# Cross-attention and soft mixture of experts: slot embeddings in the first steps, row scores between projections, key and query tiles in 104 rows, experts' weights behind the moves

## The chip, the cores and the metric

The kernel runs on one core of a Trainium2 chip. The metric is the device time of one execution in microseconds (us). TensorE (PE in the profile) multiplies, VectorE (DVE), ScalarE (ACT) and GpSimd (POOL) work on tiles, and SP only issues transfers. ACT and POOL issue transfers as well. The profile calls the loading of a stationary operand PEld.

## The reference

There are 16 batches of 100 query rows and 361 context rows of width 256. First `x = x + attention(layernorm(x), ctx, ctx)` with 16 heads of 16, then `x = x + ffn(layernorm(x))`, where the second part is a soft mixture of 16 experts with 64 slots each:

```python
q = query @ wq + bq;  k = key @ wk + bk;  v = value @ wv + bv
score = einsum('bhqd,bhkd->bhqk', q, k) / sqrt(HD) + (1.0 - mask) * -1e9
context = einsum('bhqk,bhkd->bhqd', softmax(score, -1), v)
x = x + context @ wo + bo
# ffn
x = _layernorm(x, norm_g, norm_b)
se = _layernorm(slot_embeds, slot_g, slot_b) * scale
logits = einsum('bnd,esd->bnes', x, se)
dispatch = softmax(logits, axis=1)
combine = softmax(logits over all e, s)
slots = einsum('bnd,bnes->besd', x, dispatch)
gate = gelu(slots @ Wg + bg);  up = slots @ Wu + bu
eout = (gate * up) @ Wd + bd
out = einsum('bns,bso->bno', combine, eout)
```

## The kernel before, in words

The program has three phases.

**Attention.** It is a pipeline over batches. Step t (from -3 to 17) works on several batches at once: keys and queries of batch t+3, values of t+2, row scores of t+1, probabilities of t, output of t-1. Each step has 24 slots, and a table gives the slot of every piece: `AT` for t from 0 on, `AT_FILL` for the three fill steps -3, -2 and -1. Every engine runs its own list in this order and waits on semaphores. Precision is kept by splitting values in a high and a low part, so keys and queries go out to DRAM (`k_parts`, `q_parts`) and come back as tiles `kt` and `qt`, in which one head of each half takes 48 rows of parts, 2 of mask and 2 of the maximum. The two halves (c = 0, 1) lie at rows 0 and 64.

Row scores (`scores(r)`, L697, tile `at_rows`) multiply one pair of heads, one matmul for each half in its own 50 rows; DVE takes the maximum (`head_max`, L485); after eight pairs the maxima are transposed, split and moved into rows of `qt` (`max_rows`, L257). Column scores (`scores_t`, L709, tile `at_cols`) then use all 116 rows at once, and ACT takes the exponential (`p_f`, L626), splits it (`p_h`, L631, and POOL `p_l`, L391), and PE multiplies by the values (L729).

Slot embeddings: their inputs are issued on SP in step -2 (`later_inputs`, L312 to L315); DVE takes the statistics in step 12 (L460 to L466) and normalises in step 13 (L473); POOL multiplies and adds the gains in steps 13 and 14 (L415, L418); PE transposes them in step 15 (L835) and ACT copies them (`seT`, L671).

**Routing** computes the logits and both softmaxes for each batch and is not touched but for `norm_g` and `norm_b`, which it reads.

**Experts.** Eight pairs of experts, each in two halves of the batch (h) and two experts (e): 32 units. A unit is gate and up (L1454), down (L1493), and between them slots of the next half (L1421) and combines of the previous half (L1428). DVE adds the bias into `eo` in two parts (g = 0, 1; L1359), SP moves `eo` to `eo_pair` (L1258), and the combine of the next half reads `eo_pair` after its first two gate-and-up blocks. POOL issues the weights of the next pair: `wd` and `bd` (L1164, L1165) when the last eo part is there, `wgu` (L1159) when the low parts of the former ones are made.

## Time and profile before

| | us |
|---|---|
| median of 3 runs | 1232.62 |
| lowest, highest | 1227.69, 1235.58 |
| the profiled execution, its own time | 1230.74 |
| its span | 1229.0 |
| mean granted TensorE clock | 0.934 |

The span is cut in three phases by lines: attention from 0 to 381 us, routing to about 528 us, experts to the end. The page shows busy time of each engine, and the same in 40 slices of 30.7 us, with the granted clock in tenths of 2.4 GHz. PE is busy for 89% of the span. "Idle before" in brackets is the time the engine stood still before a row and who released it.

### The profile page before, as it was taken

The page shows a single profiled execution, that of the slowest core. Times are in us where ns is not written, and L with a number is a line of the kernel's source. Part 1 is how long each engine was busy: PE and PEld are TensorE (multiplying, and loading weights), DVE is VectorE, ACT ScalarE, POOL GpSimd, SP SyncE. Part 2 cuts the span into 40 slices and gives each one's busy share as a digit, 9 for nine tenths or more (in the row PEclk, how much of TensorE's full clock was granted, in tenths as well). Part 3 has the DMA queues.
Part 4 walks back from the last instruction along what each step waited for, and adds up shares of the span by engine and source line. Part 5 has one row for each costly group of instructions (what it writes and reads, how often), then busy time and mean ns, then how long its engine had stood idle before and what let it go on. Part 6 is the DMA issues. An engine that isn't in the chain of part 4 may idle for free.

```text
span 1229.0 us, 22101 instructions
## 1 busy us (share of the span) xinstructions
PE 1094.6 (89%) x7172; PEld 865.6 (70%) x7172; DVE 701.0 (57%) x1250; ACT 576.1 (47%) x1079; POOL 344.7 (28%) x351
## 2 busy tenths in 40 slices
PE   5389899999785888789989989899899899999996
PEld 3256666666562544478878878788788788888885
DVE  5246677777734888644545645555555545555443
ACT  2147678778553888733323333333324334343321
POOL 5137777668772533210010100100100100100000
PEclk8659999999857999889999989999999999999998
DMA  7836576667301634432142232422422331423022
GB/s 176 193 73 167 134 158 164 150 147 165 81 1 35 172 101 107 124 126 62 39 124 72 60 103 70 100 82 63 133 70 55 107 87 38 124 70 75 20 62 71
DMA packets 114565, 121.74 MB, mean 99 GB/s; under 512 B 45096, under 2 KB 105188, under 8 KB 114516
## 3 DMA queue, kind: packets, MB, share of 16 engines
q1 hardware_dynamic: 102188, 80.69, 27.7%
q0 software_dynamic: 10688, 39.62, 10.7%
q10 hardware_dynamic: 1640, 0.80, 0.3%
q8 instruction: 28, 0.46, 0.2%
q14 instruction: 21, 0.17, 0.1%
HBM read 74.13 MB, written 29.93 MB: 85 GB/s over the span
## 4 chain that ended last, share of the span: by engine, by line
PE 53%; issue 3%; DVE 1%; ACT 1%; DVEq 0%; ACTq 0%
PE down L1493 15%; PE gate L1454 14%; PE up L1454 14%; PE mix L1428 5%; PE mix L1421 5%; DVE gate_sb L1336 0%; ACT hid_h L1399 0%; DVE hid_l L1341 0%; DVE slot_l L1309 0%; DVE wd_l L1347 0%; ACT gate_sb L1395 0%; ACT slot_h L1379 0%; DVE x L1318 0%; DVEq L1545 0%; DVEq L1335 0%
## 5 line engine op out<-in xcount | busy, mean ns | idle before, releaser
L1395 ACT ACTIVATE gate_sb<-gate,bgu 128x512 f32<-128x512 f32 x128 | 88.1, 688 | 249.8 <-PE gate L1454 236.3
L391 POOL TENSOR_TENSOR p_l<-p_f,p_h 121x800 f16<-121x800 f32 (+1 forms) x96 | 163.3, 1719 | 89.8 <-ACT p_h L631 89.8
L1399 ACT ACTIVATE hid_h<-gate_sb 128x512 fp32r<-128x512 f32 x128 | 80.9, 632 | 183.2 <-DVE gate_sb L1336 183.2
L1336 DVE SCALAR_TENSOR_TENSOR gate_sb<-up,bgu,gate_sb 128x512 f32<-128x512 f32 x128 | 96.0, 750 | 116.5 <-PE up L1454 110.6
L485 DVE TENSOR_REDUCE head_max<-at_rows 100x2 f32<-100x722 f32 x128 | 116.4, 909 | 63.6 <-PE at_rows L697 63.6
L1493 PE MATMUL down<-wd_h,hid_h 128*128 128x256 f32 x512 | 150.7, 294 | 0.6 <-DVE hid_l L1341 0.6
L1493 PE MATMUL down<-wd_h,hid_l 128*128 128x256 f32 x512 | 144.8, 283 | 0.0
L1493 PE MATMUL down<-wd_l,hid_h 128*128 128x256 f32 x512 | 144.7, 283 | 0.0
L1341 DVE TENSOR_TENSOR hid_l<-gate_sb,hid_h 128x512 fp32r<-128x512 f32 x128 | 88.7, 693 | 94.2 <-ACT hid_h L1399 94.2
L626 ACT ACTIVATE p_f<-at_cols 121x800 f32<-121x800 f32 (+1 forms) x96 | 79.8, 831 | 52.9 <-PE at_cols L709 51.0
L1164 POOL DMA_DIRECT2D wd<-in_Wd x16 | 12.2, 764 | 321.9 <-DVE eo L1359 301.5
L1493 PEld LDWEIGHTS down<-wd_h,hid_h 128*128 128x128 f32 x512 | 98.0, 191 | 3.3 <-issue 1.0
L1493 PEld LDWEIGHTS down<-wd_l,hid_h 128*128 128x128 f32 x512 | 98.0, 191 | 0.8
L1493 PEld LDWEIGHTS down<-wd_h,hid_l 128*128 128x128 f32 x512 | 98.0, 191 | 0.0
L1359 DVE TENSOR_TENSOR eo<-down,bd 128x512 f32<-128x512 f32 x64 | 44.3, 692 | 92.7 <-PE down L1493 92.7
L1428 PE MATMUL mix<-eo_pair,comb 128*100 128x256 f32 x256 | 70.2, 401 | 27.0 <-issue 27.0
L1454 PE MATMUL gate<-slot_h,wgu_h 128*128 128x512 f32 x256 | 92.8, 444 | 1.4 <-DVE slot_l L1309 1.4
L631 ACT ACTIVATE p_h<-p_f 121x800 f16<-121x800 f32 (+1 forms) x96 | 83.6, 871 | 3.0
L1454 PE MATMUL gate<-slot_h,wgu_l 128*128 128x512 f32 x256 | 82.3, 403 | 0.0
L1454 PE MATMUL gate<-slot_l,wgu_h 128*128 128x512 f32 x256 | 81.7, 401 | 0.0
L1454 PE MATMUL up<-slot_h,wgu_h 128*128 128x512 f32 x256 | 81.7, 401 | 0.0
L1454 PE MATMUL up<-slot_l,wgu_h 128*128 128x512 f32 x256 | 80.7, 396 | 0.0
(144 smaller groups left out, 2282.3 us busy)
## 6 DMA issues: line engine op xcount, KB each, us to landing
eo_pair<-eo SPq DMA_DIRECT2D x64, 256.0 KB, 3.7
k_parts<-kq_n SPq DMA_DIRECT2D x16, 724.0 KB, 4.2
kt<-k_parts SPq DMA_DIRECT2D x32, 362.0 KB
wgu<-in_Wg POOLq DMA_DIRECT2D x16, 512.0 KB, 7.9
wgu<-in_Wu POOLq DMA_DIRECT2D x16, 512.0 KB, 8.7
wd<-in_Wd POOLq DMA_DIRECT2D x16, 512.0 KB, 6.1
combine<-combT SPq DMA_DIRECT2D x16, 400.0 KB, 4.2
dispatch<-dispT SPq DMA_DIRECT2D x16, 400.0 KB
```

Of the source, the lines that this page charges most:

```text
L391: nc.gpsimd.tensor_tensor(p_l[i][0:kn, :, 0:N], p_f[i][0:kn], p_h[i][0:kn, :, 0:N], ALU.subtract).then_inc(p_low, 1)
L485: nc.vector.tensor_reduce(head_max[:, :, r], rows_ps[0:N, :, 0:S], AX.X, ALU.max).then_inc(max_ready, 1)
L626: nc.scalar.activation(p_f[u][0:kn].rearrange("k (g e) n -> k g (e n)", g=2), cols_ps[0:kn, :, 0:4 * N], ACT.Exp, scale=1.0 / SCALE_INV).t ...
L631: nc.scalar.activation(p_h[u][0:kn, :, 0:N], p_f[u][0:kn], ACT.Copy).then_inc(p_hi, 1)
L1336: nc.vector.scalar_tensor_tensor(gate[c % 2][:], up_ps[c % 2][:], bu_col(bgu, pair, e, c), gate[c % 2][:], ALU.add, ALU.mult).then_inc(hid ...
L1341: nc.vector.tensor_tensor(hid_l[:, c, :], gate[c % 2][:], hid_h[:, c, :].bitcast(F32), ALU.subtract).then_inc(hidl_ready, 1)
L1395: nc.scalar.activation(gate[c % 2][:], gate_ps[c % 2][:], ACT.Gelu, bias=bg_col(bgu, pair, e, c)).then_inc(gelu_ready, 1)
L1399: nc.scalar.activation(hid_h[:, c, :], gate[c % 2][:], ACT.Copy).then_inc(hidh_ready, 1)
L1421: mm = nc.tensor.matmul(mix_ps[r % 2][:, i * P:(i + 1) * P], xn_all[:, b, m * P:(m + 1) * P], disp[:, b, :], start=True, stop=True)
L1428: mm = nc.tensor.matmul(mix_ps[1 - r % 2][0:N, i * D:(i + 1) * D], comb[:, BH * h + j, :], eo_pair[h][:, j, :], start=True, stop=True)
L1454: mm = nc.tensor.matmul(bank[:], wt[e][:, kc, i, c * P:(c + 1) * P], st[h][:, kc, e, :, :].rearrange("p b s -> p (b s)"), start=(k == 0), ...
L1493: mm = nc.tensor.matmul(down_ps[t // 2][:, t % 2, :], ht[:, c, t * P:(t + 1) * P], wt[:, c, :], start=(c == 0 and k == 0), stop=(c == FC - ...
```

## The change

Six edits.

1. Slot embeddings move to the fill. The embeddings are loaded on POOL's queue before step -3, gains as one value per partition on ACT's queue, DVE takes the statistics at the end of step -3, POOL the root there, DVE normalises at the end of step -1, PE transposes into `at_out`, and ACT applies gain and bias in eight copies of 128x256 as it empties it.
2. `x` of the later batches is loaded before the mask is stored; `norm_g` and `norm_b` in step 2.
3. In `AT_FILL` the row scores go to slots 0 to 7, and the transposed maxima to slot 8.
4. Tiles `kt` and `qt`: the second half lies at row 50, the four rows of maxima at 100 to 103. A row score reads rows 0 to 99 of both (the other half's rows of `qt` are zero there).
5. Small moves between engines: the value bias is spread by ACT at the end of step -3, ACT waits for the biases only at its first key copy, and one memset of `kt` instead of two in each buffer.
6. Experts: `eo` is moved in halves g, each with its own semaphore; the combine waits for the first halves before r = 0 and for the second before r = 2; POOL issues `wgu` of the next pair only after the last moves of the pair before.

```diff
-TILE = 64
 ROW_MASK = 3 * HD
-ROW_MAX = ROW_MASK + 2
-ROWS_A = ROW_MAX
-ROWS_B = TILE + ROW_MAX + 2
+HEAD_ROWS = ROW_MASK + 2
+ROWS_A = 2 * HEAD_ROWS
+ROWS_B = ROWS_A + 4
+SET_FROM = ROWS_A // 32 * 32
...
-    "rows": (11, 12, 13, 14, 15, 16, 17, 18), "maxT": 19, "max_parts": 19,
+    "rows": (0, 1, 2, 3, 4, 5, 6, 7), "maxT": 8, "max_parts": 8,
...
         load_ctx(2, 2)
+        sp.dma_start(x_all[:, 4:B], x[4:B].rearrange("b n d -> n b d")).then_inc(x_in[1], 16)
         sp.wait_ge(mask_done, 1)
...
-            if t == -2:
-                later_inputs()
...
+        pool.dma_start(slot[:], a["slot_embeds"].rearrange("(j two) s d -> (two s) j d", two=2)).then_inc(slot_in, 16)
...
             if t == -3:
                 probability_pads()
-                value_bias()
+                slot_embeddings()
+            if t == -2:
+                bias_through_output()
             if t == -1:
-                bias_through_output()
-            if t == B - 4:
-                slot_embeddings()
-            if t == B - 3:
                 slot_normalised()
...
-            if t == B - 1:
+            if t == -1:
+                act.wait_ge(slot_gain, 1)
                 for g in range(SC // 2):
                     act.wait_ge(seT_done, g + 1)
-                    nc.scalar.activation(seT[:, :, 2 * g * P:(2 * g + 2) * P], rows_ps[:, g % 2, :].rearrange("p (c s) -> p c s", c=2),
-                                         ACT.Copy).then_inc(seT_ready, 1)
+                    for c in range(2):
+                        nc.scalar.activation(seT[:, c, 2 * g * P:(2 * g + 2) * P], out_ps[g % 2][:, 2 * c * P:(2 * c + 2) * P], ACT.Identity,
+                                             scale=slot_sb[:, 0, c:c + 1], bias=slot_sb[:, 1, c:c + 1]).then_inc(seT_ready, 1)
...
                 for c in range(2):
-                    rows = slice(TILE * c, TILE * c + ROWS_A)
-                    mm = nc.tensor.matmul(rows_ps[0:N, c, 0:SW], q[rows, r, N * c:N * c + N], k[rows, r, :], start=True, stop=True)
+                    mm = nc.tensor.matmul(rows_ps[0:N, c, 0:SW], q[0:ROWS_A, r, N * c:N * c + N], k[0:ROWS_A, r, :], start=True, stop=True)
...
-                    for odd in range(2):
-                        sp.dma_start(dst[:, :, odd, :], eo[e][odd * SL:(odd + 1) * SL]).then_inc(eo_moved[h][e], 16)
+                    for g in range(2):
+                        sp.wait_ge(eo_ready, 2 * u + g + 1)
+                        sp.sem_inc(waited, 1)
+                        if not first and g == 0:
+                            sp.wait_ge(comb_done, 4 * (2 * pair + h - 1))
+                        for odd in range(2):
+                            sp.dma_start(dst[:, 2 * g:2 * g + 2, odd, :], eo[e][odd * SL:(odd + 1) * SL, 2 * g:2 * g + 2]).then_inc(eo_moved[h][e][g], 16)
...
                     pool.wait_ge(wl_ready[e], pair + 1)
+                    if not first:
+                        pool.wait_ge(eo_moved[1][e][1], 32 * pair)
                     pool.sem_inc(waited, 1)
                     load_gate_up(pool, a, keep, e, pair + 1)
...
+                            if r % 2 == 0:
+                                for x in range(2):
+                                    pe.wait_ge(eo_moved[1 - h][x][r // 2], 32 * pair + 32 * h)
                             if r == 0:
-                                for x in range(2):
-                                    pe.wait_ge(eo_moved[1 - h][x], 32 * pair + 32 * h)
                                 pe.wait_ge(comb_in, 16 * pair + 16 * h)
```

The order on SP in step -2 and at the start of step -1. Before, seven loads of later inputs stand between the queries of batch 0 (L308) and the store of the keys of batch 1 (L266):

```order
L308 DMA qt<-q_parts 16x8x100 x2
L312 DMA xn<-in_x 100x12x256
L313 DMA slot<-in_slot_embeds 128x8x256
L315 DMA slot_g<-in_slot_g 128x256
L315 DMA slot_b<-in_slot_b 128x256
L315 DMA scale<-in_scale 128x1
L315 DMA norm_g<-in_norm_g 100x256
L315 DMA norm_b<-in_norm_b 100x256
L266 DMA k_parts<-kq_n 128x4x362
```

With the change the store follows the queries at once:

```order
L293 DMA kt<-k_parts 16x8x362 x2
L306 DMA qt<-q_parts 32x8x100 x2
L310 DMA qt<-q_parts 16x8x100 x2
L268 DMA k_parts<-kq_n 128x4x362
L273 DMA q_parts<-kq_n 128x4x100
```

The seven loads are gone from this place; one of them stands earlier on SP, two later, and the others on POOL and ACT.

PE in step -1 before: projections first, then the eight pairs of row scores, then the maxima.

```order
L761 MATMUL at_proj<-w_v,cx 121x256 x4
L761 MATMUL at_proj<-w_v,cx 119x256 x2
L747 MATMUL at_proj<-cx,w_k 128x361 x4
L780 MATMUL at_proj<-ident,xl 128x100 x2
L788 MATMUL at_proj<-xlT,w_q 128x100 x4
L697 MATMUL at_rows<-kt,qt 100x362 x16
L812 MATMUL at_rows<-ident,head_max 16x100
```

And with the change:

```order
L736 MATMUL at_proj<-cx,w_k 128x361 x2
L686 MATMUL at_rows<-kt,qt 100x362 x2
L736 MATMUL at_proj<-cx,w_k 128x361 x2
L686 MATMUL at_rows<-kt,qt 100x362 x2
L769 MATMUL at_proj<-ident,xl 128x100 x2
L686 MATMUL at_rows<-kt,qt 100x362 x4
L777 MATMUL at_proj<-xlT,w_q 128x100 x4
L801 MATMUL at_rows<-ident,head_max 16x100
L824 MATMUL at_out<-ident,slot 128x128 x16
```

The row scores stand between the projections, and the transposes of the slot embeddings between the maxima and step 0.

DVE in steps 12 and 13 before (the projections' low parts L531 and L538 and the maxima L485 stand behind the slot work):

```order
L545 TENSOR_SCALAR xlT<-at_proj 128x200
L460 TENSOR_SCALAR slot_g<-slot_g,scale 128x256
L461 TENSOR_SCALAR slot_b<-slot_b,scale 128x256
L463 BN_STATS slot_st<-slot 128x6 x8
L466 BN_AGGR slot_mv<-slot_st 128x2 x8
L531 SCALAR_TENSOR_TENSOR kq_n<-at_proj,bk,kq_n 128x361
```

With the change nothing stands there:

```order
L525 TENSOR_SCALAR xlT<-at_proj 128x200
L511 SCALAR_TENSOR_TENSOR kq_n<-at_proj,bk,kq_n 128x361
L518 SCALAR_TENSOR_TENSOR kq_n<-at_proj,bq,kq_n 128x100 x2
L465 TENSOR_REDUCE head_max<-at_rows 100x2 x4
```

## Rows read from the trace of the kernel before

**Rows 1.** The page: busy time, then PE, clock and traffic in 40 slices of 30.7 us

```profile
PE   5389899999785888789989989899899899999996
...
PEclk8659999999857999889999989999999999999998
...
GB/s 176 193 73 167 134 158 164 150 147 165 81 1 35 172 101 107 124 126 62 39 124 72 60 103 70 100 82 63 133 70 55 107 87 38 124 70 75 20 62 71
```

**Rows 2.** Timeline of SP in the fill: start, duration of issue, line, transfer

```profile
25.64 4.68 SPq L313 DMA_DIRECT2D slot<-in_slot_embeds  x1
30.37 4.54 SPq L315 DMA_DIRECT2D slot_g<-in_slot_g  x1
...
38.11 0.46 SPq L266 DMA_DIRECT2D k_parts<-kq_n  x1
...
46.25 1.21 SPq L288 DMA_DIRECT2D kt<-k_parts  x2
...
65.18 2.78 SPq L257 DMA_DIRECT2D qt<-max_p  x4
```

**Rows 3.** Timeline of ACT and PE in the fill

```profile
46.32 1.01 ACT L638 ACTIVATE kq_n<-at_proj,bk 128x361 fp32r<-128x361 f32 x2 [12.07 <-DMA k_parts<-kq_n]
...
52.78 0.62 PE L697 MATMUL at_rows<-kt,qt 50*100 50x362 f32 x2 [1.52 <-DVE head_max L485]
...
69.10 1.14 PE L709 MATMUL at_cols<-qt,kt 116*121 116x200 f32 x4 [0.73 <-DMA qt<-max_p]
```

**Rows 4.** Timeline of DVE and PE in steps 12 to 14

```profile
308.00 2.69 DVE L463 BATCH_NORM_STATS2 slot_st<-slot 128x6 f32<-128x256 f32 x8
...
312.23 1.12 PE L761 MATMUL at_proj<-w_v,cx 128*121 128x256 f32 x4 [1.83 <-DVE kq_n L538]
...
328.36 5.23 DVE L473 TENSOR_SCALAR slot<-slot,slot_mv,slot_rs 128x256 f32<-128x256 f32 x8
...
334.47 0.62 PE L697 MATMUL at_rows<-kt,qt 50*100 50x362 f32 x2 [5.16 <-DVE head_max L485]
```

**Rows 5.** Timeline of ACT and POOL at the end of step 15

```profile
371.25 0.83 ACT L626 ACTIVATE p_f<-at_cols 119x800 f32<-119x800 f32 x1
...
373.06 1.70 POOL L391 TENSOR_TENSOR p_l<-p_f,p_h 119x800 f16<-119x800 f32 x1 [5.45 <-ACT p_h L631]
```

**Rows 6.** Row scores at 150 to 300 us (ns, min/median/max), and timelines at full clock

```profile
L697 PE MATMUL at_rows<-kt,qt x138: 401/404/411, 150.0 to 299.4; 50*100 50x362 f32 x138
...
192.87 0.41 PE L697 MATMUL at_rows<-kt,qt 50*100 50x362 f32 x2
193.21 0.67 PE L709 MATMUL at_cols<-qt,kt 116*121 116x200 f32 x4
...
192.87 0.16 PEld L697 LDWEIGHTS at_rows<-kt,qt 50*100 50x100 f32 x2 [0.34 <-issue]
...
704.87 0.62 PE L1454 MATMUL gate<-slot_l,wgu_h 128*128 128x512 f32 x2
705.33 0.63 PE L1454 MATMUL gate<-slot_h,wgu_l 128*128 128x512 f32 x2
```

**Rows 7.** Experts: DVE's last eo of four units, PE's first combine, POOL's loads, PE's waits

```profile
612.66 0.69 DVE L1359 TENSOR_TENSOR eo<-down,bd 128x512 f32<-128x512 f32 x1 [0.75 <-PE down L1493]
...
768.41 0.69 DVE L1359 TENSOR_TENSOR eo<-down,bd 128x512 f32<-128x512 f32 x1 [0.75 <-PE down L1493]
...
788.80 0.69 DVE L1359 TENSOR_TENSOR eo<-down,bd 128x512 f32<-128x512 f32 x1 [0.75 <-PE down L1493]
...
1154.19 0.69 DVE L1359 TENSOR_TENSOR eo<-down,bd 128x512 f32<-128x512 f32 x1 [0.75 <-PE down L1493]
...
710.79 2.02 PE L1428 MATMUL mix<-eo_pair,comb 128*100 128x256 f32 x4 [3.44 <-issue]
...
702.29 0.76 POOL L1164 DMA_DIRECT2D wd<-in_Wd  x1 [19.07 <-DVE eo L1359]
...
1050.68 0.76 POOL L1164 DMA_DIRECT2D wd<-in_Wd  x1 [20.47 <-issue]
...
PE mix L1428 <- issue: 27.0, 7, 5.7
```

More of the change, by code:

```diff
@@ L279, in load_keys @@
             if t < 0:
[L280 removed]
+                sp.wait_ge(kt_set[i], 1)
             for c in range(2):
[L282 removed]
+                rows = slice(HEAD_ROWS * c + ROW_MASK, HEAD_ROWS * c + HEAD_ROWS)
                 sp.dma_start(kt[i][rows, :, :].bitcast(F32), at(mask_dram, p).rearrange("r (o k) -> r o k", o=1).broadcast_to([2, NPAIR, SW])
@@ L307, in load_queries @@
                 high = q_dram[i][c, 0, :, 0:N].rearrange("(d h) n -> d h n", d=HD)
-                sp.dma_start(qt[i][TILE * c:TILE * c + HD, :, cols].bitcast(F32), high).then_inc(kq_in[i], 16)
-        def later_inputs():
-            sp.dma_start(x_all[:, 4:B], x[4:B].rearrange("b n d -> n b d")).then_inc(x_in[1], 16)
-            sp.dma_start(slot[:], a["slot_embeds"].rearrange("(j two) s d -> (two s) j d", two=2)).then_inc(slot_in, 16)
-            for t, n, rows in ((slot_g, "slot_g", P), (slot_b, "slot_b", P), (scale, "scale", P), (keep["norm_g"], "norm_g", N), (keep["norm_b"], "norm_b", N)):
-                sp.dma_start(t[:], a[n].partition_broadcast(rows)).then_inc(slot_in, 16)
+                sp.dma_start(qt[i][HEAD_ROWS * c:HEAD_ROWS * c + HD, :, cols].bitcast(F32), high).then_inc(kq_in[i], 16)
         def fill_step(b, t):
@@ L333, in step @@
                 return
+            if t == 2:
+                for n in ("norm_g", "norm_b"):
+                    sp.dma_start(keep[n][:], a[n].partition_broadcast(N)).then_inc(norm_in, 16)
             if 0 <= t + 2 < B:
@@ L409, in step @@
                 residual(4 * t + 4, 4 * t + 8)
-            gain, bias = (v[:].rearrange("p (o d) -> p o d", o=1).broadcast_to([P, SC, D]) for v in (slot_g, slot_b))
-            if t == B - 3:
-                pool.wait_ge(slot_norm, SC)
-                pool.wait_ge(slot_gain, 2)
-                nc.gpsimd.tensor_tensor(slot[:], slot[:], gain, ALU.mult).then_inc(slot_scaled, 1)
-            if t == B - 2:
-                pool.wait_ge(slot_scaled, 1)
-                nc.gpsimd.tensor_tensor(slot[:], slot[:], bias, ALU.add).then_inc(slot_ready, 1)
         steps(pool, step)
@@ L427, in _ @@
         dve.memset(mask_p[:, :, S:SW].bitcast(F32), 0.0).then_inc(pad_set, 1)
-        for c in range(2):
-            dve.memset(kt[0][TILE * c + 32:TILE * c + TILE, :, :].bitcast(F32), 1.0).then_inc(kt_set[0], 1)
+        dve.memset(kt[0][SET_FROM:P, :, :].bitcast(F32), 1.0).then_inc(kt_set[0], 1)
         def mask_parts():
@@ L594, in _ @@
         act.dma_start(bo[:], a["bo"].partition_broadcast(N)).then_inc(vec_in, 16)
+        with nc.allow_non_contiguous_dma(reason="two small vectors, one value per partition"):
+            act.dma_start(slot_gb[:, 0, :], a["slot_g"].rearrange("(c p) -> p c", p=P)).then_inc(gains_in, 16)
+            act.dma_start(slot_gb[:, 1, :], a["slot_b"].rearrange("(c p) -> p c", p=P)).then_inc(gains_in, 16)
+        act.dma_start(scale[:], a["scale"].partition_broadcast(P)).then_inc(gains_in, 16)
         act.wait_ge(keep["ident_set"], 1)
         nc.scalar.activation(warm[:], neg_half[:], ACT.Exp)
-        act.wait_ge(bias_in, 32)
-        act.wait_ge(pad_set, 2)
         def part(s, b, t, trip):
@@ L634, in part @@
                     if s == tab["k_hi"][c]:
+                        if t == -3 and c == 0:
+                            act.wait_ge(bias_in, 32)
+                            act.wait_ge(pad_set, 2)
                         act.wait_ge(k_done, 2 * p + c + 1)
@@ L1225, in expert_phase @@
     down_done, eo_ready = sem("down_done"), sem("eo_ready")
-    eo_moved = [[sem(f"eo_moved{h}{e}") for e in range(2)] for h in range(2)]
+    eo_moved = [[[sem(f"eo_moved{h}{e}{g}") for g in range(2)] for e in range(2)] for h in range(2)]
     comb_done, acc_ready = sem("comb_done"), sem("acc_ready")
@@ L1497, in step @@
             if last:
-                for x in range(2):
-                    pe.wait_ge(eo_moved[1][x], 32 * pair + 32)
                 for r in range(4):
+                    if r % 2 == 0:
+                        for x in range(2):
+                            pe.wait_ge(eo_moved[1][x][r // 2], 32 * pair + 32)
                     pe.wait_ge(acc_ready, 4 * (2 * pair + 1) + r - 1)
```

60 lines of the change are left out of this document (27 added, 33 removed).

## The prediction, made before the run

> **What bounds the kernel now.** I read the page's slices first, then the timelines of the stretches in which they dip, then the expert units one by one. In the slices [rows 1] PE is at 9 tenths in the steady attention (slices 4 to 10, 92 to 307 us) and in the experts (from slice 18). It dips at the fill (slices 1 to 3), where the clock falls as well, at the end of attention (slices 11 to 13, clock down to 5 tenths, the lower of the two levels), and in routing, which the change leaves alone. So the steady loops are bound by PE, and time is to be had where PE waits. There are three such places, and the change touches all of them.
>
> **Fill.** From 25.6 us to 38.1 SP issues later inputs: slot embeddings 4.68, slot_g 4.54, and four smaller ones [rows 2], with x just before them. Behind them stands the store of batch 1's keys, issued at 38.11 and back only at 46.25. ACT waited 12.07 us for that store [rows 3]. Then come the projections, and after them eight pairs of row scores, one at a time, each with 1.5 us of PE standing still for the maximum [rows 3], until the maxima leave at 65.18 and the first column scores start at 69.10.
>
> With the change SP is free at about 25 us. But x (100x12x256, 1.2 MB) is now queued ahead of the mask's store, and slot embeddings (128x8x256, 1.0 MB) share the engines with it. The best slice moves 193 GB/s [rows 1], by which 2.2 MB are 11.5 us at worst; since these engines have a gap of a few us ahead of 25 us, I take a delay of 3.5 us to the first key store, bounded by 0 and 11.5. The tiles of batch 0 then land at about 33 us, the store of batch 1 is issued at 30 behind them and lands at 37.5 instead of 46.2. The row scores run from 33 us on, between the projections; the key copies can go at 37.5, and the chain of keys, queries and the last three pairs takes 5.6 + 3 x 1.6 = 10.4 us. Maxima leave at 48 instead of 65.2: 17 us less. Behind that comes new work: DVE's eight normalisations, 5.23 us as before [rows 4], and the last group of transposes and copies, about 1 us. Row scores of step 0 wait for it. That gives back 5.5 us, and the first column scores stand at 57 instead of 69. **Fill: 12 us less**, between 5 (the delay at its worst) and 17 (the slot work fits beside waits for the maxima's transfer). The statistics at the end of step -3 take DVE some 3.3 us in place of the spreading of the value bias, an estimated 1 us more than that, and lie within the time in which SP's loads are awaited. The bias product on PE moves one step earlier and costs about 1 us in the same cover.
>
> **End of attention.** In step 12 the statistics (2.69 us, and some 1.2 more for the gains and the aggregation beside them) stand ahead of the keys' low part, and PE waits 1.83 us for it [rows 4]. The clock falls thereafter. In step 13 the normalisation holds the maxima for 5.23 us, and PE waits 5.16 [rows 4]. In step 15 ACT does the last exponential at 371.25, after the transposes and their copies, and POOL waits 5.45 us for its split [rows 5]; the whole output of batch 15 hangs on it. All this work leaves. What is late next is the ordinary pace of the steps: row score, maximum, exponential. Idle time 1.8 + 5.2 + 5.4 = 12.4; the clock at 5 tenths in slice 11 makes PE's work there twice as long, and without the gaps it falls later. I take 3.5 us for that, between 0 and 9. **End: 16 us less**, between 12 and 21. POOL's two slot products lie beside ACT's work and count nothing; what they cover is only POOL idle.
>
> **Experts.** An undisturbed unit takes 788.80 - 768.41 = 20.39 us. From 612.66 to 1154.19 there are 25 units, 541.5 us, where 25 x 20.39 = 509.8: 31.7 us too many [rows 7]. They come at the start of each pair: PE stands before the first combine (3.44 us at 710.79) for a move that shares the engines with wd, bd and four wgu loads, and works at the lower clock afterwards (its four matmuls there take 2.02 us). PE waits so 7 times, 27.0 us in sum; one of them is the 5.7 at the very end. In one pair of the seven it did not wait: there POOL issued wd 1.4 us late (20.47 against 19.07 us idle [rows 7]), so the moves were ahead of the weights.
>
> The change gives just this lead. The first combine needs only the parts g = 0, which DVE finishes 1.44 us before g = 1 (0.75 idle and 0.69 of work in each of the eo rows), and their moves are issued before wd is. The g = 1 parts are wanted two blocks later, over 10 us. Moreover wgu waits for the moves; it is used three units or some 60 us later, and behind it on POOL stands the load of the next dispatch weights, which waits for PE's slots of the second half, over a unit later, anyhow; so this wait costs nothing. SP issues twice as many moves, each under a microsecond like its other issues, and idles otherwise. So all 31.7 us go, and at the end the first combine can start some 2 us earlier. **Experts: 33 us less**, between 22 (a third of the waits stay) and 36.
>
> **Row scores in 100 rows.** The two matmuls of a pair last 404 ns each and 410 ns together, so they start together, one in each half of the rows; what follows starts 0.34 us after [rows 6]. With the change both use the same rows and must follow each other. How long one takes on the full array I read from the gate: 0.46 us for two of 512 columns [rows 6], 0.23 each; by columns 362 are 0.163, a pair 0.33. That is the same 0.34. So side by side they gained nothing. **Zero**, with the ends: 0.34 each, that is 0.34 x 128 pairs = +43.5 us, and -0.16 us a pair, the exposed weight load, that is -20 us. I take the gate's row because type and form are nearest. The Trainium skill ("TensorEngine Tiling (Array Packing)", Theoretical Speedup) gives up to twice the speed for row tiling with 64 rows or fewer, which speaks against this edit; by it a pair would go from 0.34 to 0.68. The trace does not bear out that a pair now is faster than two in a row.
>
> The column scores lose 12 rows and no columns. The two norm loads in step 2 are 1.8 us of SP issue where SP is not waited for. Nothing for either.
>
> **Sum.** 12 + 16 + 33 = 61. The profiled execution took 1230.7 us (1.9 under the median): **1170 us**.
>
> **Rivals.**
>
> A. The halves of the rows did run side by side to some use, and a pair now takes 0.68 us: +43.5, so 1213. For it: both start together. Against: the gate's row. Chance 0.08.
>
> B. The change from halves to whole array costs PE something at each pair, and goes. For it: the weights of a pair are not loaded ahead, 0.16 us in which PEld had been idle for 0.34 [rows 6]. If that whole time is saved at 128 pairs, 20 us: 1150. Chance 0.10. The skill's same page (Key Properties) says that a change of tiling mode drains TensorE; by that rule this rival would be the likeliest, but the row gives a ceiling only.
>
> C. The moves are late all the same, since wd's packets overtake even the first halves: the 31.7 us stay, 1202. Against: the pair at 1050. Chance 0.08.
>
> D. The early x and slot loads push out the first stores so far that the fill gives nothing: 1182. Chance 0.05.
>
> E. Slower: the clock in the steady attention. Slices 4 to 10 are 215 us at 9 tenths [rows 1], and the row scores change their form there, as does the spacing of work at the loop's start. If PE stays at 1.2 GHz, each us of its work takes two. From 61 / 215 = 28% of that stretch at the lower level on, the change is slower than before; a full stretch would give 1385. Against: PE is busy throughout, and the clock was back at 9 tenths by slice 3 before, from the same fill. Chance 0.03, at 1250 or so.
>
> The forecast has 0.66, with its own range of 1155 to 1185. From 1150 to 1202 lie the forecast, half of B, C and D, 0.84 in sum. A measurement of this kernel tells 1% from no change; 1% below the median is 1220. A lies just within "faster", so faster is 0.94, within 1% 0.03 (A together with a lost fill or C), slower 0.03.
>
> **What would show it.** SP stores batch 1's keys by 31 us and loads them by 39; first column scores at 54 to 60 us. No gap before row scores in step 14; the last exponential directly behind the column scores. No PE wait at L1428's successor at pair starts, and each unit 20.4 us. Row pairs: next instruction 0.33 to 0.35 us behind. Wrong would be: the mask's store landing after 22 us; PE waiting before the first combine; a start-to-start time of pairs above 0.4 us; slices 4 to 10 with a clock below 9.

## The result

| | before | changed |
|---|---|---|
| median of 4 runs, us | 1234.05 | 1179.87 |
| lowest, highest | 1227.69, 1235.58 | 1176.21, 1180.30 |
| profiled execution, its span | 1230.74, 1229.0 | 1179.72, 1178.0 |
| mean granted TensorE clock | 0.934 | 0.955 |

The ratio is 0.9564 with a 95% interval of 0.9524 to 0.9604: faster by 4.4%. The forecast was 1170 us, between 1150 and 1202 (1155 to 1185 as its own range); the measured time lies in both, 10 us above the forecast.

The page of the changed kernel, as in [rows 1] (slices of 29.4 us now):

```profile
span 1178.0 us, 22243 instructions
...
PE   5588899999886888789999999999999999999997
...
PEclk8689999999956999979999999999999999999999
...
GB/s 204 165 112 155 136 158 154 148 172 142 123 1 36 164 104 108 126 156 64 41 116 89 41 129 73 78 109 71 133 81 54 111 91 40 129 73 55 44 61 78
```

In the fill the third slice has the clock at 8 tenths, where it was at 5; at the end of attention one slice, the twelfth, has it at 5 tenths in both kernels.

**Where the time went.** A mark that both kernels have is the moment at which SP issues a step's maxima (`qt<-max_p`); others are the first instruction of routing (DVE's statistics of `x`) and the last `eo` of the first pair of experts, which is the fourth unit.

| mark | before | changed | gained since the mark above | forecast |
|---|---|---|---|---|
| maxima issued in step 0 | 87.07 | 78.55 | 8.5 | 12 (fill) |
| maxima issued in step 12 | 307.36 | 301.96 | -3.1 | 0 (row pairs) |
| routing begins | 381.26 | 364.39 | 11.5 | 16 (end of attention) |
| last `eo` of the first pair | 612.66 | 596.56 | -0.8 | 0 |
| end of the span | 1229.0 | 1178.0 | 34.9 | 33 (experts) |

The sum is 51.0, where 61 were forecast. Three terms fell short, by 3.5, 3.1 and 4.5 us, 0.8 us were lost in routing and the first pair, and the largest term came 1.9 us above what was worked out.

**Experts.** POOL's rows at the start of a pair (start, time, line, transfer; idle before in brackets), against [rows 7]:

```profile
679.53 0.76 POOL L1153 DMA_DIRECT2D wd<-in_Wd  x1 [19.06 <-DVE eo L1351]
...
681.23 0.72 POOL L1148 DMA_DIRECT2D wgu<-in_Wg  x1 [0.41 <-issue]
...
685.73 0.71 POOL L1148 DMA_DIRECT2D wgu<-in_Wg  x1 [3.06 <-issue]
```

PE's waits from 540 us to the end (line waited for, us in sum, times, longest), where [rows 7] has 27.0, 7, 5.7:

```profile
PE mix L1420 <- issue: 2.5, 1, 2.5
```

Only the wait at the very end is left, 2.5 us instead of 5.7, and every unit from the third to the thirtieth takes 20.39 to 20.42 us (the second and the last two are shorter in both kernels, 19.4 and 18.6 us). Before, the first units of the last seven pairs took 26.96, 26.66, 25.57, 24.05, 25.86, 20.39 and 24.66 us. The first combine of a pair is of ordinary speed as well, PE's timeline in the changed kernel (the second row is the end of the program):

```profile
602.82 1.03 PE L1420 MATMUL mix<-eo_pair,comb 128*100 128x256 f32 x4
...
1166.76 5.67 PE L1420 MATMUL mix<-eo_pair,comb 128*100 128x256 f32 x16 [2.52 <-issue]
```

The landings show the mechanism. At this pair start SP issues the four moves of the last unit at 595.90, 596.54, 597.35 and 597.99, and POOL issues `wd` at 597.86. The three moves ahead of `wd` land 2.4 us after their issue, the one behind it after 6.2 us, at 604.14. That is after the first combine (602.82), which does not need it; it is read only at 623.21. Before, the move that was issued just behind `wd` (614.09) landed at 623.62. In the one pair that did not wait, both moves stood ahead of `wd` and landed within 3.9 us.

That POOL issues `wgu` of the next pair only after the last moves of the pair before holds for half of `wgu`. The program waits for each expert's own moves, and those of the first expert landed a unit earlier. So at the pair start above two loads go right behind `wd`, at 681.23 and 681.94, and only the other two wait, until 685.73.

**Fill.** SP's timeline (start, time on the queue, line, transfer), against [rows 2]:

```profile
5.88 0.49 SPq L241 DMA_DIRECT2D xn<-in_x  x1
9.39 6.64 SPq L243 DMA_DIRECT2D mask_parts<-mask_p  x1
16.15 4.20 SPq L249 DMA_DIRECT2D qt<-one_rows  x6
25.73 0.41 SPq L268 DMA_DIRECT2D k_parts<-kq_n  x1
...
34.73 0.59 SPq L268 DMA_DIRECT2D k_parts<-kq_n  x1
...
41.69 1.21 SPq L290 DMA_DIRECT2D kt<-k_parts  x2
...
54.99 0.39 SPq L268 DMA_DIRECT2D k_parts<-kq_n  x1
...
56.41 3.13 SPq L259 DMA_DIRECT2D qt<-max_p  x4
```

The first row is the early load of `x`. The mask's store behind it takes SP 6.64 us and lands 16.3 us after its issue, at 25.7 us; before, it landed after 3.3 us. The program lets SP store no keys until the mask has landed, and that is what SP waits for last (line waited for, us in sum, times, longest, up to 60 us):

```profile
SPq L268 <- DMA mask_parts<-mask_p: 5.3, 1, 5.3
```

So the first keys are stored at 25.73 where it was 16.4 before, though DVE has them ready at 16.3 us in both kernels. Batch 1's store is at 34.73 (before 38.11, forecast by 31), the maxima at 56.41 (before 65.18, forecast 48). Then DVE and PE:

```profile
55.94 5.97 DVE L453 TENSOR_SCALAR slot<-slot,slot_mv,slot_rs 128x256 f32<-128x256 f32 x8
```

```profile
39.73 0.92 PE L686 MATMUL at_rows<-kt,qt 100*100 100x362 f32 x2 [5.76 <-DMA qt<-q_parts]
...
58.09 1.09 PE L824 MATMUL at_out<-ident,slot 128*128 128x128 f32 x4 [3.23 <-DVE slot L453]
...
62.99 1.09 PE L824 MATMUL at_out<-ident,slot 128*128 128x128 f32 x4 [0.35 <-ACT seT L661]
63.73 0.80 PE L686 MATMUL at_rows<-kt,qt 100*100 100x362 f32 x2
...
65.94 0.57 PE L698 MATMUL at_cols<-qt,kt 104*121 104x200 f32 x4
```

PE waits for tiles until 39.73, and from 56 to 63.7 the slot work holds the row scores of step 0, in part while the maxima are on their way. From the maxima's issue to the first column scores 9.5 us go by, where it was 3.9 before. Column scores start at 65.94, only 3.2 us earlier than before. That the gain is 8.5 at step 0's maxima comes with the clock. Windows of the timeline (busy time of PE, PEld, DVE, ACT, POOL, then the clock, DMA share and GB/s) from the first column scores to the maxima, in the changed kernel

```profile
65.94:78.55 12.61, 10.00 (x84) 7.82 (x84) 8.72 (x14) 10.27 (x15) 9.28 (x7) 0.97 0.46 89
```

and in the kernel before:

```profile
69.10:87.07 17.97, 16.24 (x84) 10.81 (x85) 8.06 (x14) 10.91 (x15) 9.31 (x7) 0.59 0.58 123
```

The same 84 matmuls take 12.6 us at a granted clock of 0.97, where they took 18.0 at 0.59: 5.4 us. Why the clock came back sooner was not tried. For later comparisons, the window from 60 to 90 us in the changed kernel:

```profile
60.00:90.00 30.00, 26.01 (x212) 20.60 (x213) 18.06 (x34) 21.62 (x35) 14.37 (x12) 0.87 0.49 117
```

**Row pairs.** PE's and PEld's timelines in the steady attention, against [rows 6]:

```profile
162.07 0.57 PE L686 MATMUL at_rows<-kt,qt 100*100 100x362 f32 x2
162.49 0.57 PE L698 MATMUL at_cols<-qt,kt 104*121 104x200 f32 x4
...
162.07 0.25 PEld L686 LDWEIGHTS at_rows<-kt,qt 100*100 100x100 f32 x2 [0.23 <-DVE head_max L465]
...
209.40 0.58 PE L686 MATMUL at_rows<-kt,qt 100*100 100x362 f32 x2 [0.37 <-DVE head_max L465]
209.81 1.03 PE L793 MATMUL at_proj<-w_o,attT 128*100 128x256 f32 x4
```

and in the kernel before, a pair that is followed by the same four matmuls of the output projection:

```profile
198.08 0.41 PE L697 MATMUL at_rows<-kt,qt 50*100 50x362 f32 x2 [0.16 <-DVE head_max L485]
198.42 1.11 PE L804 MATMUL at_proj<-w_o,attT 128*100 128x256 f32 x4
```

What follows a pair starts 0.42 us after it; it was 0.34. But the four matmuls behind it now take 1.03 us instead of 1.11, so that pair and projection together take 1.44 us, where it was 1.45. With column scores behind it is 0.99 instead of 1.01 [rows 6]. By these rows the work of PE has not become longer. What has is the way from a pair's start to its end, 0.57 us instead of 0.41, and so the maximum comes later. A usual step takes 17.93 us instead of 17.77, and PE now waits for maxima, by its waits from 180 to 284 us in the changed kernel

```profile
PE at_rows L686 <- DVE head_max L465: 4.2, 17, 0.4
```

and in the kernel before:

```profile
PE at_rows L697 <- DVE head_max L485: 1.1, 6, 0.2
```

**End of attention.** PE's timeline of step 14, and its windows of 5 us:

```profile
321.63 0.57 PE L686 MATMUL at_rows<-kt,qt 100*100 100x362 f32 x2 [2.04 <-DMA kt<-k_parts]
```

```profile
320.00:325.00 5.00, 2.37 (x22) 2.00 (x23) 1.82 (x2) 0.37 (x1) 1.95 (x3) 0.86 0.03 5
325.00:330.00 5.00, 4.77 (x37) 3.85 (x34) 2.93 (x6) 3.43 (x5) 3.07 (x2) 0.50 0.00 0
```

The 5.16 us behind the normalisation are gone [rows 4], but 2.04 us for a key tile stand in their place, and the granted clock falls to 0.50, which is 1.2 GHz, behind it (PE did 2.37 us of work in these 5 us). POOL's rows of the last step, against [rows 5], show the last two splits with no gap beyond the usual 0.33 to 0.35 us:

```profile
354.24 1.71 POOL L388 TENSOR_TENSOR p_l<-p_f,p_h 119x800 f16<-119x800 f32 x1 [0.33 <-ACT p_h L613]
356.28 1.71 POOL L388 TENSOR_TENSOR p_l<-p_f,p_h 119x800 f16<-119x800 f32 x1 [0.34 <-ACT p_h L613]
```

### The profile page after: what moved, and what is told of

It is laid out like the page before. It is cut to its first block, busy times and chain, and to the rows that moved or that the text cites. A ratio compares the mean times of both kernels' runs of the same rounds, so it can differ in the third digit from the quotient of the medians.

```text
span 1178.0 us, 22243 instructions
## 1 busy us (share of the span) xinstructions
PE 1068.8 (91%) x7172; PEld 873.0 (74%) x7172; DVE 696.9 (59%) x1247; ACT 576.8 (49%) x1084; POOL 332.0 (28%) x348
## 4 chain that ended last, share of the span: by engine, by line
PE 55%; DVE 1%; issue 1%; ACT 0%; DVEq 0%; ACTq 0%
PE down L1486 15%; PE gate L1446 15%; PE up L1446 15%; PE mix L1413 5%; PE mix L1420 5%; DVE gate_sb L1328 0%; ACT hid_h L1391 0%; DVE hid_l L1333 0%; DVE wd_l L1339 0%; DVE slot_l L1301 0%; DVE x L1310 0%; ACT gate_sb L1387 0%; ACT slot_h L1371 0%; DVEq L1539 0%; DVEq L1327 0%
## 5 line engine op out<-in xcount | busy, mean ns | idle before, releaser
L686 PE MATMUL at_rows<-kt,qt 100*100 100x362 f32 x256 | 81.4, 400 | 21.9 <-DVE head_max L465 13.7
L1446 PE MATMUL up<-slot_h,wgu_l 128*128 128x512 f32 x256 | 80.1, 394 | 0.0
```

The source lines that it names most:

```text
L686: mm = nc.tensor.matmul(rows_ps[0:N, c, 0:SW], q[0:ROWS_A, r, N * c:N * c + N], k[0:ROWS_A, r, :], start=True, stop=True)
L1446: mm = nc.tensor.matmul(bank[:], wt[e][:, kc, i, c * P:(c + 1) * P], st[h][:, kc, e, :, :].rearrange("p b s -> p (b s)"), start=(k == 0), ...
```

## The experiments

All edits are made to the changed kernel (e7, e10, e11, e12 combine them), and all ratios are to the kernel before on the same chip. Kernels e1 to e4 shared one set of its runs, e5 to e8 another, e9 to e12 a third. The changed kernel's own is 0.9564 [0.9524, 0.9604], from runs of its own.

### The experts: halves or the weights' wait?

**e1** leaves the weights' wait out.

```diff
-                    if not first:
-                        pool.wait_ge(eo_moved[1][e][1], 32 * pair)
                     pool.sem_inc(waited, 1)
```

> The changed kernel, but POOL issues wgu without waiting for the moves. Theory: the waits of PE went because the first halves of eo are moved 1.4 us ahead of wd; the weights' wait adds nothing. Then every first unit of a pair still takes 20.4 us and the time stays at 1178 to 1182. Rival: wgu, 2 MB, is what delayed the moves, and its wait removed the stalls. Then first units are back at 24 to 27 us and the time rises by 15 to 31 us, to 1195 to 1211.

Measured: 1177.13 us (1176.13 to 1179.97), 0.9568 [0.9519, 0.9618], as the theory has it. The third to the thirtieth unit take 20.4 us each, and no combine but the last waits. The weights (`wgu`) land 7.1 us after their issue instead of 5.8, for which nothing waits.

**e2** issues all moves of a unit when both halves are there, and PE waits for all of them before r = 0, also at the end of the program (not shown); the weights' wait stays.

```diff
-                        sp.wait_ge(eo_ready, 2 * u + g + 1)
+                        sp.wait_ge(eo_ready, 2 * u + 2)
...
-                            if r % 2 == 0:
-                                for x in range(2):
-                                    pe.wait_ge(eo_moved[1 - h][x][r // 2], 32 * pair + 32 * h)
                             if r == 0:
+                                for x in range(2):
+                                    for g in range(2):
+                                        pe.wait_ge(eo_moved[1 - h][x][g], 32 * pair + 32 * h)
```

> The changed kernel, but SP issues all four moves of a unit only when both parts of eo are there, and PE waits for all of them before the first combine; POOL still waits with wgu for the moves. Theory (the lead of the first halves did it): the stall that wd and bd alone cause is back, as at the last pair of the kernel before (that unit 24.66 us, 4.3 too many): seven times 3 to 5 us, and 2 to 3 at the very end, in sum 23 to 38, so 1203 to 1218. Rival (the wait of wgu did it): first units stay at 20.4 us, 1178 to 1184.

Measured: 1216.78 us (1214.46 to 1218.06), 0.9881 [0.983, 0.9931], in the theory's range, 39.7 us above e1 on the same chip and 36.9 above the changed kernel. The first units of the pairs take 28.74, 25.26, 25.83, 25.56, 24.08, 22.48 and 24.96 us. PE's waits from 540 us on, and a row of its timeline:

```profile
PE mix L1420 <- DMA eo_pair<-eo: 29.7, 8, 5.8
```

```profile
609.16 2.02 PE L1420 MATMUL mix<-eo_pair,comb 128*100 128x256 f32 x4 [5.82 <-DMA eo_pair<-eo]
```

The four moves of that unit are issued at 597.70, 598.34, 599.05 and 599.69, and land at 600.12, 604.73, 605.67 and 608.82; only the first stands ahead of `wd` (598.22). So waits and lower clock are back with the weights' wait in place. The whole gain of the experts hangs on the halves: an earlier issue, and a later need of the second half. The wait as built is worth nothing, with the halves (e1) or without them (29.7 us of waits here, 27.0 before). It holds back only half of `wgu`: here too the first expert's loads go at 599.62, while the moves are under way, and the second's at 609.54. A wait that holds back all of it was not tried.

Nor were the two parts of the halving tried apart. The landings in the changed kernel allow an estimate. There the last move lands at 604.14, 1.3 us after the first combine's start, and at the five other pair starts where it is late 0.6 to 0.8 us after, 4.7 us in sum. So waiting for all moves, but issuing them as they are ready, would cost some 5 us of waits and what the clock adds; most of the gain is the earlier issue.

### The layout of the halves

**e3** puts the halves back to rows 0 and 64, with the rows of the maxima and the memsets of `kt` that go with it (not shown), and leaves all else.

```diff
-HEAD_ROWS = ROW_MASK + 2
-ROWS_A = 2 * HEAD_ROWS
-ROWS_B = ROWS_A + 4
+HEAD_ROWS = 64
+ROWS_A = ROW_MASK + 2
+ROWS_B = HEAD_ROWS + ROW_MASK + 4
...
-                    mm = nc.tensor.matmul(rows_ps[0:N, c, 0:SW], q[0:ROWS_A, r, N * c:N * c + N], k[0:ROWS_A, r, :], start=True, stop=True)
+                    rows = slice(HEAD_ROWS * c, HEAD_ROWS * c + ROWS_A)
+                    mm = nc.tensor.matmul(rows_ps[0:N, c, 0:SW], q[rows, r, N * c:N * c + N], k[rows, r, :], start=True, stop=True)
```

> The changed kernel with tiles kt and qt as before: second half at row 64, row scores on 50 rows each. Theory: a pair on the shared 100 rows takes 0.42 us to the next instruction instead of 0.34, and of the 0.64 us a step that this makes, most comes back at the transitions; the step of the loop goes from 17.93 back to 17.77 us and the time falls by 2 to 5 us, to 1175 to 1178. Rival A: the packing helps elsewhere (fill, end), and its removal costs 1 to 5 us. Rival B: no difference that can be measured.

Measured: 1184.17 us (1179.23 to 1185.71), 0.9624 [0.9576, 0.9673]. The theory's time did not come; the numbers fit rival A or B. The usual step is back at 17.77 us, and the waits from 180 to 284 us are those of before:

```profile
PE at_rows L688 <- DVE head_max L466: 1.2, 6, 0.2
```

But in this kernel step 0 takes 26.1 us, where the changed one has 22.1. Its window:

```profile
60.00:90.00 30.00, 26.33 (x158) 17.78 (x156) 15.36 (x26) 17.77 (x29) 10.85 (x8) 0.67 0.36 79
```

So in these two traces what the packed rows cost from step 0's maxima to step 12's (219.7 us here, 223.4 with them) is offset in step 0, where the clock is 0.67 against 0.87. The intervals of the two ratios overlap a little (0.9576 to 0.9604), so they do not tell e3 from the changed kernel. On the same chip three of e3's four times (1183 to 1186) lie above all of e1 and e4 (1176 to 1180), so that the packed rows may be worth a few us in this version; in the version of e10 nothing of it is seen (e11, below).

Of the 3.7 us between these two spans 2.3 are not the layout's. In the changed kernel two steps are slow once, 21.05 and 18.43 us. e11, with the halves apart, has 21.08 and 18.62 us at the same two steps, and e1, with packed rows, has 19.40 and 18.00. Packing neither makes these slow steps nor is needed for them; what does was not found.

### The fill: x, the slot work and the order

**e4** loads `x` at the end of the fill, ahead of the maxima of step -1.

```diff
         load_ctx(2, 2)
-        sp.dma_start(x_all[:, 4:B], x[4:B].rearrange("b n d -> n b d")).then_inc(x_in[1], 16)
         sp.wait_ge(mask_done, 1)
...
             if t == -1:
+                sp.dma_start(x_all[:, 4:B], x[4:B].rearrange("b n d -> n b d")).then_inc(x_in[1], 16)
                 max_rows(b, t)
```

> The changed kernel, but x of the later batches is loaded at the end of step -1, where SP waits for the maxima anyhow. Theory: its 1.2 MB ahead of the mask's store held SP (6.64 us in that one issue) and put off the first key store from 16.4 to 25.7 us; without it that store goes at 17 to 19 us, the first row scores start 5 to 8 us earlier than 39.7, and the time falls by 4 to 7 us, to 1173 to 1176. Rival: the slot embeddings on POOL's queue hold it as much; the first key store stays after 22 us and the time within 2 us of 1180.

Measured: 1178.78 us (1176.55 to 1179.58), 0.957 [0.9522, 0.9619], no difference. The first keys are stored at 17.97 instead of 25.73, the first row scores run at 34.02, the maxima leave at 51.66 instead of 56.41. Then it is lost again:

```profile
64.24 1.13 PE L698 MATMUL at_cols<-qt,kt 104*121 104x200 f32 x4 [4.10 <-DMA qt<-max_p]
```

The maxima stand behind `x`, PE waits 4.10 us, and the granted clock from 60 to 90 us is 0.77 instead of 0.87. Step 0's maxima leave at 79.62, 1.1 us later than in the changed kernel. The theory was right for the stores and row scores and wrong for the time: the 1.2 MB had only moved to another transfer that is waited for.

**e9** takes the early load out as in e4 and loads `x` in step 0, behind the keys' tiles, where nothing small is waited for at once.

```diff
                 load_keys(b - 1, t - 1)
+            if t == 0:
+                sp.dma_start(x_all[:, 4:B], x[4:B].rearrange("b n d -> n b d")).then_inc(x_in[1], 16)
             if 0 <= t + 1 < B:
```

> The changed kernel, but x of the later batches is loaded in step 0, behind the keys of batch 2 and ahead of no transfer that is awaited (in the run with x late it stood ahead of the maxima, for which PE then waited 4.1 us). Theory: the first key store goes at 18 us, the maxima of batch 0 leave at 51.7 and PE does not wait for them; the end of step 0 moves from 78.6 to 72 to 75, and the time falls by 3 to 6 us, to 1174 to 1177. Rival: in step 0 the clock takes it, as a step at the lower level costs 5 us or more; the time stays at 1178 to 1182.

Measured: 1172.87 us (1171.28 to 1173.49), 0.9553 [0.9518, 0.9587]. SP's and PE's timelines:

```profile
9.47 0.37 SPq L242 DMA_DIRECT2D mask_parts<-mask_p  x1
...
17.91 0.39 SPq L267 DMA_DIRECT2D k_parts<-kq_n  x1
...
49.50 2.79 SPq L258 DMA_DIRECT2D qt<-max_p  x4
```

```profile
33.13 0.57 PE L687 MATMUL at_rows<-kt,qt 100*100 100x362 f32 x2 [1.04 <-DMA qt<-q_parts]
...
59.20 0.57 PE L699 MATMUL at_cols<-qt,kt 104*121 104x200 f32 x4
```

The mask's store takes SP 0.37 us instead of 6.64 and lands after 7.4 us instead of 16.3, with the slot embeddings still in flight beside it. The first row scores come 6.6 us earlier, at the 33 us of the forecast, and maxima of step -1, of step 0 and routing 6.9, 6.7 and 7.6 us. Measured against the kernel before, step 0's maxima are now 15.3 us earlier. So the place of `x` cost the change some 7 us of the trace. The time is 1 us below the theory's range. Its six times lie wholly below the four of the changed kernel (lowest 1176.21), but the two were timed against different runs of the kernel before, and the two ratios don't tell them apart. What the marks show is the stronger evidence.

**e6** does normalisation, transposes and copies of the slots at the end of step -2 instead of step -1.

```diff
                 bias_through_output()
-            if t == -1:
                 slot_normalised()
...
-            if t == -1:
+            if t == -2:
                 act.wait_ge(slot_gain, 1)
...
-            if t == -1:
+            if t == -2:
                 pe.wait_ge(bov_ready, 1)
```

> The changed kernel, but the slot embeddings are normalised, transposed and copied at the end of step -2 instead of -1, where PE waits 5.8 us and DVE 5.2 us for the loads of batch 0. Theory: the slot work after the maxima (55.9 to 64.1 us) was on the path; the row scores of step 0 start 5 to 7 us earlier than 63.7, step -1 starts at most 2 us later, and the time falls by 3 to 6 us. Rival: what follows is bound by transfers (the keys of batch 1, stored at 55 us), the step 0 takes as long, and the time stays within 2 us of 1180.

Measured: 1175.38 us (1174.08 to 1177.96), 0.9564 [0.9511, 0.9617]. Row scores start at 41.58 (39.73 in the changed kernel) and maxima leave at 57.14; the first column scores start at 61.41, 4.5 us earlier, but at a granted clock of 0.72 they and the rest of step 0 take 15.2 us instead of 12.6, and its maxima are at 76.64 instead of 78.55. So 1.9 us are left at this mark of hiding the slot work beside the tiles' wait. The span is 5.7 us shorter; the rest comes later, 2.2 us of it in the loop, for a reason that was not looked for. The median fits the theory, but the ratio is that of the changed kernel, so the times do not tell the two apart.

**e7** is e4 and e6 together, **e10** e9 and e6.

> Both: x late, and slot work at the end of step -2. If the two gains add up, 7 to 12 us under the changed kernel, 1168 to 1173. If the earlier loads of batch 0 take the gap into which the slot work was put, only 4 to 7 us, 1173 to 1176.

> The same with the slot work at the end of step -2 as well. If both add up: the end of step 0 at 69 to 73, 1168 to 1173. If the earlier loads leave no gap for the slot work: as e9 or up to 2 us better, 1173 to 1177.

Measured for e7: 1184.18 us (1180.05 to 1187.36), 0.9618 [0.9563, 0.9673]; neither expectation came. PE's waits:

```profile
PE at_cols L697 <- DMA qt<-max_p: 11.9, 1, 11.9
```

With the slot work gone from the place where e4 had it, nothing covers the `x` ahead of the maxima, and PE stands 11.9 us for them. For e10: 1173.39 us (1170.97 to 1175.14), 0.9557 [0.9522, 0.9592], the same as e9. The two savings don't add up. Maxima leave at 54.95 (e9 49.50), since with early tiles the slot work of step -2 stands in front of row scores that could run (they start at 38.20, in e9 at 33.13), and step 0's at 74.47 (e9 71.81).

**e8** puts the slot work back to steps 12, 13 and 15; POOL's part and the tile of the transposes move with it (not shown), the loads stay early.

```diff
-            if t == -1:
+            if t == B - 4:
+                slot_embeddings()
+            if t == B - 3:
                 slot_normalised()
...
-            if t == -1:
+            if t == B - 1:
                 act.wait_ge(slot_gain, 1)
```

> The changed kernel, but the slot work stands in steps 12, 13 and 15 as before (with gain and bias still applied by ACT in eight copies). Theory: it costs 4 us in step 12, 5.2 in step 13 and some 5 to 7 in step 15, and gives back what it costs in the fill, 3 to 8: 5 to 12 us slower, 1185 to 1192. Rival: the clock, which at half level made the first step long before as well, takes the fill's gain; 12 to 17 us slower.

Measured: 1189.75 us (1186.12 to 1191.87), 0.9669 [0.9613, 0.9725], in the theory's range: 9.9 us above the changed kernel and, on the same chip, 14.4 above e6. Maxima of step 0 at 77.34 (1.2 us earlier than in the changed kernel), routing at 374.16 (9.8 later). PE waits in step 14:

```profile
325.38 0.92 PE L688 MATMUL at_rows<-kt,qt 100*100 100x362 f32 x2 [3.54 <-DVE head_max L466]
```

So the move of the slot work is worth some 10 us in all: 11 at the end, for 1.2 in the fill.

**e5** puts row scores and maxima of the fill back to the steps' end; **e12** does it to e10.

```diff
-    "rows": (0, 1, 2, 3, 4, 5, 6, 7), "maxT": 8, "max_parts": 8,
+    "rows": (11, 12, 13, 14, 15, 16, 17, 18), "maxT": 19, "max_parts": 19,
```

> The changed kernel, but in step -1 the eight row scores come after the projections again, as before. Theory: in the changed kernel they run from 39.7 to 53 us beside the projections, and PE and DVE wait for transfers before; put behind, they take eight times 1.6 us after the queries' projection; maxima leave at 63 to 66 us instead of 56.4, and the time rises by 6 to 9 us. Rival: the slot work and the transfers set the start of step 0, and the order costs under 3 us.

> e10 with the row scores of step -1 behind the projections. In the changed kernel that order made no difference, since what it lost before the maxima (5.8 us) came back in step 0 by the clock and by earlier key stores (47.4 instead of 55.0 us). Theory: with the transfers earlier the order counts more, since nothing else holds the maxima: 2 to 6 us slower than e10. Rival: again no difference, within 1.5 us.

Measured for e5: 1179.92 us (1179.68 to 1180.37), 0.9594 [0.9542, 0.9646]. The maxima leave 5.8 us later (62.19), but step 0's only 3.9 later (82.47), and routing 0.7 later (365.05). Batch 2's keys are stored at 47.41 instead of 54.99, which may be why; it was not tried. The times are equal, as the rival has it. For e12: 1185.13 us (1182.77 to 1187.24), 0.9656 [0.962, 0.9691], where e10 has 0.9557 [0.9522, 0.9592] on the same chip: 11.7 us more, well above both expectations. The maxima of step -1 leave 8.4 us later (63.34), those of step 0 6.7. PE's timeline has seven waits in a row like this one, the last before the transposition of the maxima, at starts 1.93 us apart:

```profile
50.79 0.92 PE L686 MATMUL at_rows<-kt,qt 100*100 100x362 f32 x2 [1.00 <-DVE head_max L466]
```

In the changed kernel the transfers hold the row scores until 39.73, and their order says little. In e10 they can start at 38.20 beside the projections; put last (e12) they start at 46.77 and run one by one, with PE standing still between them.

**e11** is e10 with the halves at rows 0 and 64.

> e10 with the tiles as before, halves at rows 0 and 64. Theory: in the loop a step takes 17.77 instead of 17.93 us, 1 to 3 us over the attention; in the fill the packed tiles had the better clock in step 0 (78.6 against 83.9 us at its end), by 3 to 5 us. In sum 0 to 4 us slower than e10. Rival: the clock in step 0 was chance; then 1 to 3 us faster than e10.

Measured: 1174.78 us (1167.51 to 1180.89), 0.9566 [0.9523, 0.9609], not told apart from e10: the times spread too far to choose between theory and rival. The loop's step is 17.75 us, and step 0's maxima leave at 77.07 instead of 74.47.

The lowest median is that of e9. By the ratios it is not told apart from e10, e11, e6 or the changed kernel.

## Why the prediction was right, and by how much not

The sum was right to 10 us of 61. One term was right in mechanism and size, two had the right chain with a part mis-sized, and one lost what it was to leave alone. Two of the four marks that the prediction had named for being wrong came: the mask's store landed after 22 us (at 25.7), and a pair took more than 0.4 us.

**Experts, 33 forecast, 34.9 measured.** The mechanism was right: the moves go ahead of `wd`, 31.5 us of waits and lower clock at pair starts went, and the wait at the end shrank (forecast 2, measured 3.4). "This wait costs nothing" holds (e1), and it brings nothing either; the halves alone carry the term (e2). Rival C, moves late all the same, is what e2 shows without the halves, and in part it is true with them: the move behind `wd` is late at six pair starts, and only its late use hides that.

**Fill, 12 forecast, 8.5 measured, of which 5 by luck.** The chain was right, the delay of the first key store mis-sized: 3.5 taken, 9.3 measured (25.73 against 16.4), inside its bounds of 0 and 11.5. I had let the engines' spare time carry most of `x`. But SP waits for the landing of the mask's store, which took 16.3 us behind the queued 1.2 MB. The prediction had named this landing among its marks, and priced it too low. e9 returns 7.8 of the 9.3. In e9 ACT waits 3.11 us for a bias load and starts its key copies 1.5 us later than before, which is the rest. The slot work was sized well: it puts 5.6 us between maxima and column scores (9.5 against 3.9), where 5.5 were taken. At the first column scores the gain was only 3.2 us. The clock in step 0, which I had not counted, gave 5.4 us back; without it the term would have been 3 and the time about 1185, at the end of the range of 1155 to 1185. Rival D had this mechanism, but for a full loss. A reading was loose as well: of the eight pairs before, one waited 1.52 us for the maximum and the others 1.01.

**Row pairs, 0 forecast, 3.1 lost.** The pitch of a pair is 0.42 us, above the 0.4 that the prediction had named as its mark of being wrong. It is made of 0.25 us to the second matmul (PEld's two loads end then) and 0.17 behind it, where I took 0.163 for each. The 0.163 of the gate's row is right for the second; before it another 0.08 us pass, which by PEld's row go with the loading of the pair's weights. That was the step that failed in the working: it had no load in it. But the zero is nearly right for PE's own work, since the matmuls behind a pair are quicker by as much (1.44 us against 1.45 for pair and projection; in e3 the projection takes 1.11 us again). This fits a cost of the change of form, as rival B had it, but what exactly costs it was not tried, and no gain came of it. What the loop loses is 0.16 us a step, some 1.3 in the eight steps from 4 to 12, beside more waits for maxima (4.2 us against 1.1 from 180 to 284 us), and e3 gives both back. The rest of the 3.1 us are two steps that are slow once (21.05 and 18.43 us), one of them with the clock at 0.92 where PE had waited 1.42 us. They are not the layout's, by e11 and e1. That page of the Trainium skill ("TensorEngine Tiling (Array Packing)", Theoretical Speedup) gives up to twice the speed for the tiled rows. The trace shows less: the tiled pair has a pitch of 0.34 us against 0.42, and with what follows no gain; in the time of the kernel it cannot be told.

**End of attention, 16 forecast, 11.5 measured.** From step 12's maxima to step 13's 4.1 us were gained, to the last maxima 1.7, and from there to routing 5.7, against 1.8, 5.2 and 5.4 of idle time. The first and the last came in full. The first came with 2.3 us of clock, since it stayed at 1.00 from 310 to 320 us, where it had fallen to 0.86 and 0.50 behind the statistics. The step that failed is the middle one. I counted the 5.16 us behind the normalisation in full and added 3.5 for a clock that "falls later". But 2.04 us for a key tile and 1.00 for a maximum took the place of the wait, and the clock fell behind them at 325 us, as it had fallen behind the 5.16. I had named the "ordinary pace" as what is late next, and put no price on it. I had also read the page one slice off: the 5 tenths stand in slice 12 (338 to 369 us), not 11, and in the fill the clock is at 9 tenths again in slice 4, not 3. e8 confirms the size of the move from the other side, 11 us at this end.

## What to carry to other kernels

A large load that nobody waits for belongs behind the small transfers of the chain, and it has to be put where nothing small is wanted next: moved in front of another small transfer it cost the same again, only later (e4), or more (e7). If the program also waits for the landing of the small store behind it before it goes on, the delay goes straight into that wait (here 16.3 us to the landing instead of 3.3). Where an engine waits for a move that runs beside weights, first try to issue it in parts as they are ready and to wait for each part only where it is read; holding half of the weights back was worth nothing here. A time to the next instruction is not yet a cost: look at when the work behind it is done. Moving work into a stall is worth what the stall then covers and no more: here two such moves into the same stall did not add up (e10), and removing a wait of 5.16 us did not keep the clock up, as shorter waits took its place.

## What the runs showed of the hardware

- A store of 46 KB issued behind a load of 1.2 MB kept SP for 6.64 us and landed after 16.3 us; with the load elsewhere it took SP 0.37 us and landed after 7.4 (e9), and what hung on it came 7.8 us earlier.
- Two matmuls of 362 columns in 50 rows each start together and the next instruction follows after 0.34 us; on the same 100 rows the second starts after 0.25 and the next 0.17 later, 0.42 in sum. Four matmuls of 256 columns behind such a pair take 1.11 us in the first case and 1.03 in the second.
- Of four moves of 128 KB, the three issued ahead of the load of `wd` landed after 2.4 us, and the one issued 0.13 us behind it after 6.2 (changed kernel, 597.86). Where only the first stood ahead of it, the others landed after 6.4, 6.6 and 9.1 us (e2).
- The same 84 matmuls of step 0 took 12.6 us at a granted clock of 0.97, and 18.0 at 0.59.
